# Rotary halves read 64 partitions further on, with query and key rows ordered by halves, in the middle stage of a two-layer kernel

## What is computed

```python
def _apply_rope(t, cos, sin):                 # t: (batch, token, head, 16)
    t1, t2 = jnp.split(t, 2, axis=-1)         # two halves of 8 features
    rot = jnp.concatenate([-t2, t1], axis=-1)
    return t * cos[None, :, None, :] + rot * sin[None, :, None, :]

h   = _rmsnorm(x, ln1_w)
qkv = jnp.einsum('bsh,oh->bso', h, wqkv)
q = qkv[..., :NH * HD].reshape(B, S, NH, HD)                 # NH = 16, HD = 16
k = qkv[..., NH * HD:(NH + NKV) * HD].reshape(B, S, NKV, HD) # NKV = 4
v = qkv[..., (NH + NKV) * HD:].reshape(B, S, NKV, HD)
q, k = _apply_rope(q, cos, sin), _apply_rope(k, cos, sin)
```

## Time and profile before

| | |
|---|---|
| time, median of 3 runs | 2442.03 us (2441.58 to 2443.93) |
| the profiled execution | 2438.78 us, span 2436.9 us |
| TensorE busy | 2232.1 us (92%) |
| VectorE busy | 2034.2 us (83%) |
| ScalarE busy | 1549.0 us (64%) |
| GpSimd busy | 587.8 us (24%) |

### The profile page before, as it was taken

The page is one execution under the profiler, slowest core; times in us unless marked ns, Lnnn a source line. Parts: engine busy times, 40 slices in busy tenths (PEclk is TensorE's granted clock), DMA queues, the critical chain, the costliest instruction groups (busy, mean ns, idle before and its releaser), DMA issues. The chain is left out here.

```text
span 2436.9 us, 47806 instructions
## 1 busy us (share of the span) xinstructions
PE 2232.1 (92%) x15890; PEld 1286.7 (53%) x15891; DVE 2034.2 (83%) x5167; ACT 1549.0 (64%) x2981; POOL 587.8 (24%) x845
## 2 busy tenths in 40 slices
PE   4599997999999999999999999999998873899997
PEld 2355554444444544544444544444444653788886
DVE  7767756899999999999999999999991664677775
ACT  3133322578888888888888888888887551454543
POOL 5412100222112112211211211212010366433333
PEclk8799995899999999999999999999999986999999
DMA  4167764645435434322322332432023983344443
GB/s 163 65 185 213 224 193 72 104 85 105 79 80 97 74 77 92 66 60 55 72 54 55 72 61 48 72 60 68 22 80 104 306 278 145 68 80 80 80 82 69
DMA packets 168140, 246.37 MB, mean 101 GB/s; under 512 B 52120, under 2 KB 124968, under 8 KB 162100
## 3 DMA queue, kind: packets, MB, share of 16 engines
q0 software_dynamic: 38304, 112.51, 24.6%
q1 hardware_dynamic: 124596, 121.03, 16.6%
q10 hardware_dynamic: 5044, 10.32, 1.4%
HBM read 120.38 MB, written 122.36 MB: 100 GB/s over the span
## 5 line engine op out<-in xcount | busy, mean ns | idle before, releaser
L1444 ACT ACTIVATE a_p<-banks 128x512 f32<-128x512 f32 x2176 | 1131.4, 607 | 261.0 <-PE banks L1337 209.9
L1497 DVE TENSOR_REDUCE a_mx<-banks 128x1 f32<-128x512 f32 x1536 | 944.1, 682 | 25.3 <-PE banks L1326 24.9
L1405 PE MATMUL banks<-a_p,a_v 128*32 128x512 f32 (+3 forms) x5120 | 591.8, 546 | 1.5 <-ACT a_o L1462 1.1
L1326 PE MATMUL banks<-a_k,a_q 52*128 52x512 f32 (+5 forms) x1600 | 447.7, 414 | 1.9 <-DVE a_rowtop L1494 0.3
L1337 PE MATMUL banks<-a_q,a_k 50*128 50x512 f32 (+7 forms) x1600 | 417.3, 397 | 1.1
L1494 DVE CUSTOM_DVE_ANT_0 a_masked<-banks,a_later 128x512 bf16<-128x512 f32 (+3 forms) x768 | 330.9, 485 | 20.5 <-PE banks L1326 18.7
L1337 PEld LDWEIGHTS banks<-a_q,a_k 54*128 54x128 f32 (+1 forms) x1600 | 227.4, 185 | 199.9 <-DVE a_mx L1497 95.4
L1326 PEld LDWEIGHTS banks<-a_k,a_q 52*128 52x128 f32 (+1 forms) x1600 | 223.8, 185 | 119.5 <-DVE a_mx L1497 55.1
L1326 PE MATMUL banks<-a_k,q 48*128 48x512 f32 (+6 forms) x896 | 258.7, 424 | 5.4 <-DMA a_k<-aug_rows 3.8
L1337 PE MATMUL banks<-q,a_k 50*128 50x512 f32 (+7 forms) x896 | 232.0, 403 | 0.9 <-DVE a_orow L1517 0.3
L1405 PEld LDWEIGHTS banks<-a_p,a_v 128*32 128x32 f32 x5120 | 109.6, 109 | 176.8 <-issue 127.3
(11 more groups left out here) (274 smaller groups left out, 2872.0 us busy)
## 6 DMA issues: line engine op xcount, KB each, us to landing
expert_rows<-a_zeros POOLq DMA_DIRECT2D x132, 258.0 KB, 5.2
a_k<-ka_parts POOLq DMA_DIRECT2D x42, 256.0 KB, 6.3
e_x<-expert_rows SPq DMA_DIRECT2D x72, 129.0 KB, 2.6
expert_rows<-e_y SPq DMA_DIRECT2D x72, 128.0 KB, 2.0
qa_parts<-m_part SPq DMA_DIRECT2D x16, 512.0 KB, 4.3
ka_parts<-m_part SPq DMA_DIRECT2D x16, 512.0 KB, 4.5
va_tiles<-m_va SPq DMA_DIRECT2D x8, 1024.0 KB, 4.5
qb_parts<-m_part SPq DMA_DIRECT2D x16, 512.0 KB, 4.7
```

The lines of the kernel that those rows point to most:

```text
L1326: ins = pe.matmul(ps[bank][:, col:col + w], q_op[r % 3][part, p, qt * P:(qt + 1) * P], keys_of(r, k0)[part, kp, k0:k0 + w], start=True, st ...
L1405: ins = pe.matmul(ps_o[VW * h:VW * h + VW, c0:c0 + w], v_op[o][:, kt, hk * VW:hk * VW + VW], prob[:, (at + slot) % NPB, col:col + w], star ...
L1444: nc.scalar.activation(prob[:, (t * NSC + n) % NPB, :], ps[bank][:, :], ACT.Exp, scale=SCALE).then_inc(s_ex, 1)
L1497: ins = v.tensor_reduce(top, ps[bank][:, :], AX.X, ALU.max)
```

## The change

The swapped products go. TensorE makes only the plain projections of branch B: `features` 6 and 7 (256 queries) and 8 (keys), and `values` becomes number 9. For this the weight columns are put in another order first: within a group of 128, feature by feature instead of head by head (row = feature * 8 + head), so that the first halves of all heads lie in partitions 0 to 63 and the second halves in 64 to 127. GpSimd does this with six copies, once, ahead of block 0. The four key heads are doubled to fill 128 partitions. `rope` is now four operations: the product with cos on 128 partitions, the product with sin on partitions 64 to 127 of the bank written to partitions 0 to 63, the same from 0 to 63 to 64 to 127, and the sum. The tables of cos and sin have the same size in the new order. The keys' operations and store cover 128 partitions instead of 64. `features` 0 no longer waits for the copy of B's values, but for the products of the last `rope`; `features` 1 waits for the copy. The attention's loads of branch B read rows 8 apart instead of neighbouring ones, in pieces of the same size.

```diff
+            pool.wait_ge(s_w, NW * 16)
+            for k in range(KD):
+                ins = nc.gpsimd.tensor_copy(
+                    wb[:, k, D:2 * D].rearrange("p (m d h) -> p m d h", m=KD, d=HD),
+                    wb[:, k, 0:D].rearrange("p (m h d) -> p m d h", m=KD, d=HD))
+            ins.then_inc(s_zero, 1)
+            pool.wait_ge(s_zero, 1)
+            for k in range(KD):
+                for r in range(2):
+                    ins = nc.gpsimd.tensor_copy(
+                        wb[:, k, 0:P].rearrange("p (d r h) -> p d r h", d=HD, r=2)[:, :, r, :],
+                        wb[:, k, 2 * D:2 * D + KV * HD].rearrange("p (h d) -> p d h", d=HD))
+            ins.then_inc(s_zero, 1)
             pool.wait_ge(s_h, 1)
...
-                pe.wait_ge(s_pd, blk * NDVE + 1)
-                for n in range(2):
-                    features(n, wa, n * P, P, xT)
+                pe.wait_ge(s_pd, max(blk * NDVE, 1))
+                features(0, wa, 0, xT)
+                pe.wait_ge(s_pd, blk * NDVE + 1)
+                features(1, wa, P, xT)
...
-                features(6, wb, 0, P, hT)
+                features(6, wb, D, hT)
...
-                features(7, wb, D, P, hT)
+                features(7, wb, D + P, hT)
                 if more:
                     turn_xn(blk + 1)
                 pe.wait_ge(s_pd, blk * NDVE + 2)
-                features(8, wb, P, P, hT)
-                pe.wait_ge(s_pd, blk * NDVE + 3)
-                features(9, wb, D + P, P, hT)
+                features(8, wb, 0, hT)
                 if more:
                     turn_h(blk + 1)
-                pe.wait_ge(s_pd, blk * NDVE + 4)
-                features(10, wb, 2 * D, KV * HD, hT)
-                features(11, wb, 2 * D + KV * HD, KV * HD, hT)
                 if ahead:
                     pe.wait_ge(s_xT, blk * KD + 2 * KD)
                     pe.wait_ge(s_hT, blk * KD + 2 * KD)
                     first_products(blk + 2)
-                pe.wait_ge(s_pd, blk * NDVE + 5)
-                values(12, wb, 2 * D + 2 * KV * HD, KV * HD, hT, range(TPB))
+                pe.wait_ge(s_pd, blk * NDVE + 3)
+                values(9, wb, 2 * D + 2 * KV * HD, KV * HD, hT, range(TPB))
...
-                    dve.wait_ge(s_pr, blk * 13 + (r + 1))
-                    ch.did(v.tensor_tensor(xf[i][0:n, :], ps[BANK[a % 4]][0:n, :], cos[0:n, tok:tok + BT], ALU.mult))
-                    v.tensor_tensor(rot[0:n, :], ps[BANK[r % 4]][0:n, :], sin[0:n, tok:tok + BT],
+                    dve.wait_ge(s_pr, blk * NPR + (m + 3))
+                    ch.did(v.tensor_tensor(xf[i][:, :], from_[:, :], cos[:, tok:tok + BT], ALU.mult))
+                    ch.did(v.tensor_tensor(rot[0:HALF, :], from_[HALF:P, :], sin[0:HALF, tok:tok + BT], ALU.mult))
+                    v.tensor_tensor(rot[HALF:P, :], from_[0:HALF, :], sin[HALF:P, tok:tok + BT],
                                     ALU.mult).then_inc(s_pd, 1)
+                    ch.settle()
...
-                    eng.dma_start(q_op[o][at:at + HD, :, :].bitcast(F32),
-                                  q_d[PROD_Q[n], ds(tb * (GH * HD), GH * HD), :].rearrange(
-                                      "(p j d) t -> j d p t", p=PAIRS, j=2)[j]).then_inc(q_sem, 16)
                 if second:
+                    eng.dma_start(q_op[o][at:at + HD, :, :].bitcast(F32),
+                                  q_d[PROD_Q[n], ds(tb // 2 * P, P), :].rearrange(
+                                      "(d g p j) t -> g j d p t", g=2, p=PAIRS, j=2)[g % 2, j]).then_inc(q_sem, 16)
```

More of the change, by code:

```diff
@@ L515, in middle @@
         NDVE = 6
+        NPR = 10
         BANK = [6, 7, 4, 5]
@@ L551, in _ @@
             nc.gpsimd.memset(vb[:, :, :, :], 0.0).then_inc(s_zero, 1)
-            pool.wait_ge(s_zero, 1)
+            pool.wait_ge(s_zero, 3)
             nc.gpsimd.memset(va[:, :, :, HD:HD + 1], 1.0)
@@ L588, in _ @@
                     sp.wait_ge(s_lo, blk * NS + (m + 1))
[L589 to L595, removed]
+                    dram = (M["qa_d"], M["qa_d"], M["ka_d"], M["ka_d"], M["qb_d"], M["qb_d"], M["kb_d"])[m]
+                    row = b * D + (m % 2) * P if m < 6 else b * P
+                    sp.dma_start(dram[:, row:row + P, tok:tok + BT].rearrange("a f t -> f a t"),
+                                 part[m][:, :, :].bitcast(F32)).then_inc(s_pst[m], 16)
                 sp.wait_ge(s_va, blk * 2 + 2)
@@ L643, in turn_h, with features @@
                     ins.then_inc(s_ht, 1)
-            def features(n, w, at, m, src):
+            def features(n, w, at, src):
                 for c in range(KD):
-                    ins = pe.matmul(ps[BANK[n % 4]][0:m, :], w[:, c, at:at + m], src[:, c, :],
+                    ins = pe.matmul(ps[BANK[n % 4]][:, :], w[:, c, at:at + P], src[:, c, :],
                                     start=(c == 0), stop=(c == KD - 1))
@@ L683, in both @@
                 for n in range(2, 4):
-                    features(n, wa, n * P, P, xT)
+                    features(n, wa, n * P, xT)
                 pe.wait_ge(s_lo, blk * NS + 1)
@@ L688, in both @@
                 values(5, wa, 2 * D, D, xT, (2, 3))
+                if blk == 0:
+                    pe.wait_ge(s_zero, 2)
                 pe.wait_ge(s_lo, blk * NS + 3)
-                features(6, wb, 0, P, hT)
+                features(6, wb, D, hT)
                 pe.wait_ge(s_lo, blk * NS + 4)
-                features(7, wb, D, P, hT)
+                features(7, wb, D + P, hT)
                 if more:
@@ L756, in high @@
                 def high(m):
-                    n = P if m < 6 else KV * HD
                     if m < 4:
-                        act.wait_ge(s_pr, blk * 13 + (m + 1))
+                        act.wait_ge(s_pr, blk * NPR + (m + 1))
                     else:
@@ L859, in low @@
                 def low(m):
-                    n = P if m < 6 else KV * HD
-                    high = part[m][0:n, 0, :].bitcast(F32)
+                    high = part[m][:, 0, :].bitcast(F32)
                     dve.wait_ge(s_hi, blk * NS + (m + 1))
@@ L867, in low @@
                     else:
[L868 removed]
+                        ins = v.tensor_tensor(part[m][:, 1, :], xf[(blk % 2 * NS + m) % 2][:, :], high, ALU.subtract)
                     ins.then_inc(s_lo, 1)
                 def rope(m):
[L873 removed]
+                    rot, from_ = rots[m % 2], ps[BANK[(m + 2) % 4]]
                     i = (blk % 2 * NS + m) % 2
[L875 to L876 removed]
                     dve.wait_ge(s_lo, blk * NS + (4 if m < 6 else 5))
[L878 to L880 removed]
+                    dve.wait_ge(s_pr, blk * NPR + (m + 3))
+                    ch.did(v.tensor_tensor(xf[i][:, :], from_[:, :], cos[:, tok:tok + BT], ALU.mult))
+                    ch.did(v.tensor_tensor(rot[0:HALF, :], from_[HALF:P, :], sin[0:HALF, tok:tok + BT], ALU.mult))
+                    v.tensor_tensor(rot[HALF:P, :], from_[0:HALF, :], sin[HALF:P, tok:tok + BT],
                                     ALU.mult).then_inc(s_pd, 1)
+                    ch.settle()
                     dve.wait_ge(s_pd, blk * NDVE + m)
[L883 removed]
+                    v.tensor_tensor(xf[i][:, :], xf[i][:, :], rot[:, :], ALU.add).then_inc(s_xf, 1)
                 if more:
@@ L896, in both @@
                 if blk == 0:
-                    dve.wait_ge(s_zero, 2)
+                    dve.wait_ge(s_zero, 4)
                 dve.wait_ge(s_vst, blk * 32 + 16)
                 for q in range(2):
-                    dve.wait_ge(s_pr, blk * 13 + (5 + q))
+                    dve.wait_ge(s_pr, blk * NPR + (5 + q))
                     for i in range(2):
@@ L2387, in constants @@
     ang = (np.arange(L, dtype=np.float32)[:, None] * inv[None, :]).astype(np.float32)
[L2388 to L2391, removed]
+    emb = np.repeat(np.concatenate([ang, ang], axis=1).T, P // HD, axis=0)
+    sign = np.where(np.arange(P) < HALF, -1.0, 1.0).astype(np.float32)[:, None]
+    c["c_cos"] = np.cos(emb).astype(np.float32)
+    c["c_sin"] = (np.sin(emb) * sign).astype(np.float32)
     slope = np.array([2.0 ** -0.5 * (2.0 ** -0.5) ** i for i in range(HEADS)], np.float32) / np.float32(SCALE)
```

14 lines of the change are left out of this document (9 added, 5 removed).

## The result

The changed kernel takes 2450.07 us (median of 11 runs, 2444.45 to 2452.69), the kernel before 2442.03 (11 runs): a ratio of 1.003, interval 1.0022 to 1.0039. That is 8.0 us slower, where 1.2 us slower was forecast. Timed again on another chip it was 1.0022 (1.0013 to 1.0031), 4.2 us. The profiled execution took 2452.38 (span 2450.5). All times in the text are us.

What follows compares the result with a forecast made beforehand. A loop through VectorE, ScalarE and TensorE was taken to bound the middle blocks, not TensorE's work. Terms -4.3 - 3.0 - 0.5 + 9.0 gave +1.2 us on 2442.03, so 2443.2, range 2433 to 2453.

Steps and rivals of the forecast that it cites:

- likeliest case: Whole kernel: 2443.2 us, own range 2439 to 2448 (a clock fall worth 0.8 to 2.3), 50 in 100.
- -7.8: Whole kernel without the clock's loss: gains of 4.3, 3.0 and 0.5 us, giving 2434.2.
- The bound: Middle blocks: a loop through VectorE, ScalarE and TensorE decides the 31.45 us block, not TensorE's summed work.
- Rival 1: Middle blocks: TensorE is the bound, the loop looser; blocks of 28.5 us, time 2420; 5 in 100.
- The idle piece: Ahead of `first_products`, blocks 0 to 5: TensorE's freed time becomes 3.2 us of idle in one piece.
- The clock's term, 9.0: Blocks 0 to 5: idle ahead of `first_products` brings a clock fall each, 1.5 us lost per block, 9.0 in all.
- rival 3: Ahead of `first_products`: the clock stays low for longer, 3.0 us lost per block, +10.2 in all, 2452.2; 21 in 100.
- The loop's gain, -4.3: Copy to `first_products`: 0.3 us gained in each of blocks 1 to 3, 1.1 in blocks 0, 4 and 5.
- Blocks 6 and 7, -3.0 and -0.5: Last two blocks: 3.0 us gained at `features` 1 of block 7, then 0.5 within block 7.
- The later landing: Stage end: the keys' 512 KB store lands after 4.7 us, not 3.1, eating what block 7 wins.
- What costs nothing: GpSimd's copies (0 to 1.8 us), offset products, 128-partition keys, attention loads and `settle`: all taken as free.
- the sum: Whole kernel: -4.3 - 3.0 - 0.5 + 9.0 = +1.2 us, 2443.2 as median.

Runs made afterwards that it cites:

- filler: The changed kernel plus 14 transposes of the identity on TensorE ahead of `first_products`: 2436.32 us, 0.9981 of the kernel before; on a second chip 2439.09, 0.9966.
- after again: The changed kernel, unaltered, timed once more on chip C: 2443.5 us, 1.0022 of the kernel before.
- both moves: The changed kernel with `values` ahead of `first_products` and ScalarE taking the turned h before `high(5)`, no filler: 2408.0 us, 0.9867 of the kernel before.

## Why the prediction was right and where it was off

The time lay in the range of 2433 to 2453, and the mechanism was the forecast's: the loop, not TensorE's work, sets the block, and the freed time turns into idle that costs the clock. The time lay above the likeliest case's 2439 to 2448, and the size was 7 us off. The sign is worth little: +1.2 was what was left of -7.8 and +9.0, and slower had 0.30 against 0.25 for faster. Step by step, at the last copy:

- **The bound.** Right. Rival 1 (blocks of 28.5) did not come, though TensorE's work shrank by what was counted; it came (28.0) once two moves cut the loop.
- **The idle piece.** Forecast 3.2 us, ended by ScalarE's L756: 3.61, by L756.
- **The clock's term, 9.0.** This is the mis-sized step. The runs show 13.3: 1.66 in block 0, then 2.1, 2.4, 2.5, 3.0 and 1.6 in blocks 1 to 5 (the changed kernel's block less that of the kernel with filler). I took block 0's fall as the pattern for all; in blocks 1 to 4 half clock lasted twice as long, which was rival 3, priced at 3.0 each with 21 in 100. The truth was a mixture of rival 3 and the likeliest case. Half clock also reached past the first part of `first_products`, since L83 starts while it is still low (214.20, 4.18 instead of 3.60). The estimate from the Trainium skill's figure ("TensorE: Matmul & The Clock Gate", section "HAM oscillation — how this bites in real kernels"), 5.0, was further off than 9.0; the measurement decides.
- **The loop's gain, -4.3.** Measured with the clock held (filler against before): blocks 1 to 3 in sum -0.07 where -0.9 was forecast, blocks 4 and 5 -0.94 and -0.93 where -1.1 each was; block 0 gave 0.52 (`first_products` at 143.71 less 0.35 for a later start of the whole, against 143.88), not 1.1. In all -2.5. In block 2 `first_products` was forecast 24.0 behind the copy (206.52 - 182.52), against 24.26 before; it was 24.39 with the clock held. What failed is the pitch: 0.61, 0.61, 0.72 were taken for a rope, 0.72, 0.73, 0.79 came, 0.3 more for each of two ropes, which the wait of `low(1)` and the handovers gave back in part. The row I went by was that of an instruction that starts at the same partition as the last, and `settle`, taken as free, may be the sum's 0.07.
- **Blocks 6 and 7, -3.0 and -0.5.** -0.77 and -3.24 at the copies, -4.0 together; the 3.0 was counted at `features` 1 of block 7, so most of it shows in block 7. The later landing did not eat the end: the keys' stores of 512 KB landed after 2.8 in the median of eight, not 4.7, and the last was issued 7.15 later than before, as late as the copy. Transfers of the changed kernel, columns as in the earlier trace rows:

```profile
kb_parts<-m_part SPq DMA_DIRECT2D x8, 512.0 KB, 2.8
```

- **What costs nothing.** Right: GpSimd's copies were under cover, though they took 2.6 us where at most 1.8 was given; its idle ahead of the zeroing shrank from 11.69 to 9.11. `low(1)`'s wait for ScalarE was gone.

-2.5 - 4.0 + 13.3 = +6.8, with the later start of 0.35 the 7.15 of the last copy.

Errors of +4.3 (clock), +1.8 (loop), -0.5 (blocks 6 and 7) and 0.35 (start) make the 5.95 by which the last copy missed the sum.

What stays open: why half clock lasted 3.5 us in some blocks and 7 in others; and the part behind the last copy. The medians and the last copies differ by up to 5 us in both directions (after again: +9.25 at the copy, +4.2 in time; both moves: -26.3 and -31.3). In the profiled executions the part behind the last copy took 2080.2 and 2068.9 for one and the same changed kernel, and 2073.8 for the kernel before. So the traces can't say whether the attention, which reads rows 8 apart now, gains or loses some us; no experiment was made on it.

## What to carry to other kernels

Work taken from the engine that looks full gains nothing while a loop of handovers through other engines is as long; follow one iteration in order of time and cut the loop first, by letting its short link go ahead of the long one. Here the same edit that lost 4 to 8 us then gained 24. Ask of every freed microsecond on TensorE whether it becomes one long idle piece ahead of dense work on the critical loop, and price that by all falls of the trace, the long ones too. While the clock falls behind such a piece, a loop made shorter by 0.52 gave 0.07 in one block: look at the clock before you count a gain on the loop.

## What was not expected of the hardware

- The clock's loss behind idle pieces of 3.60 to 3.61 us (blocks 1 to 5) varied from 1.6 to 3.0 us: 3.5 to 4 us at 0.50 or some 7, begun earlier or later in the idle piece.
- Matmuls of no use in the idle piece took 11.6 us off the way from the first copy to the last. With a loop that leaves no such piece they gave nothing: 0.9887 (0.9869 to 0.9904) with them, 0.9867 (0.9853 to 0.9881) without, each against before on its own chip, which does not show that they cost.
- VectorE's product at an offset of 64 partitions lasts as long as one without (0.69), but starts 0.11 to 0.14 later.
- The keys' stores of 512 KB, the last of that size in each block, landed after 2.8 us in the median, the queries' of the same size after 4.7.
